# Retention in chunks worked as two spans of 64 tokens, with the outer product ahead of the scores and two GpSimd additions tied to the state

## The chip, the cores and the metric

One core of one Trainium2 chip runs the whole kernel in one launch. The metric is the device time in microseconds, the median of several runs. Five engines work side by side: TensorE (PE in the rows, its weight loads PEld), VectorE (DVE), ScalarE (ACT), GpSimd (POOL) and SyncE (SP, which issues DMAs). They meet only at semaphores.

## The reference, cut to what matters

A feed-forward block with 16 routed experts stands on both sides of an attention block; the change is inside the attention block, which has two layers over 4 sequences of 1024 tokens, 256 features, 16 heads of 16.

```
for i in range(2):
    ln_x = layer_norm(x, ln1_g[i], ln1_b[i])
    q, k, v, xo = split(ln_x @ proj_w[i] + proj_b[i], 4)
    scores = einsum('bhld,bhmd->bhlm', q, k) * D      # D[h,l,m] = gamma_h ** (l - m), 0 where m > l
    ret = einsum('bhlm,bhmd->bhld', scores, v)
    ret = (ret * silu(xo)) @ reto_w[i] + reto_b[i]
    x = x + ret
    h = layer_norm(x, ln2_g[i], ln2_b[i])
    x = x + gelu(h @ ffn1_w[i] + ffn1_b[i]) @ ffn2_w[i] + ffn2_b[i]
```

The decay is a power of the distance, so a sequence can be cut into pieces: inside a piece the scores are masked and multiplied with the values; what came before the piece is held in a state, the decayed sum of key times value, which is multiplied with the queries.

## The kernel before, in words

The 4096 tokens are 8 tiles of 512; with two layers there are 16 steps, and `step(a)` of each engine works on tile `a` and on the tile before it, `b`. Two steps make one sequence (`a.j` is 0 or 1); each tile is cut into four chunks `c` of 128 tokens, and `k` counts the eight chunks of a sequence. The order of work is written out by hand, engine by engine, in the five `step` functions; a semaphore says when each piece is done.

For chunk `c`, TensorE turns the keys (`turn_keys`, 2 transposes), makes the scores of the *next* chunk (`scores`, 8 matmuls that each use 32 rows of the array, so that four stand side by side in it), then `retain` (per half of the features 4 matmuls of the old state with the queries and 8 of the masked scores with the values, each 32 columns wide, again four side by side), then `outer` (8 matmuls, keys times values, the addition to the state), and then some blocks of the feed-forward layer of tile `b` (`feed_in`, 8 blocks a step, dealt out by `FEEDS`). The chunk matmuls are in full float32, and each leaves two rows in the trace; the others are split by `split3` into three fp32r products on the whole 128x128 array. A step ends with `turn_a`, `feed_out`, `project_out`, `project` of the next tile, its first `scores`, `turn_b` and `project_values`.

VectorE copies the turned keys out of PSUM (`copy_keys`), masks the scores (`masked`, four instructions a chunk), makes the new state (`update_state`: one product with a mask, two multiply-adds), applies the gate (`gate_result`) and makes the low parts of the feed-forward activations (`low_feed`). `turn_keys` of chunk `c+1` waits for the state of chunk `c`, since keys and products lie in the same PSUM bank, `m_ps`.

GpSimd makes `b_lo`, which `feed_in` of block 0 waits for, and right behind it adds two biases to the residual (`add_bias`).

Of the kernel before, what the change touches and what calls it, by code (L numbers as in the profile page):

```python
# [73 lines left out]
PH = QUAD // HD  # L74
WEIGHT_PIECES = 2 * KD + 3
# [1667 lines left out]
def retention(nc, h_sb, ident, eps, ins, x_dram, home, first_moe, next_moe, held, x_stored):  # L1743

    tag = "l"
    with ExitStack() as ctx:
# [28 lines left out]
        fresh = sb("fresh", [P, KD, P])  # L1775
        odd_probs = sb("probs1", [P, H * P])
# [4 lines left out]
        probs = [sb("probs0", [P, H * P]), odd_probs]  # L1781
# [15 lines left out]
        ret_ps, m_ps = rm_ps[:, 0, :], rm_ps[:, 1, :]  # L1797
# [14 lines left out]
        ret_done, gated_done, st_done, fresh_done, state_done = (  # L1812
            sem("ret_done"), sem("gated_done"), sem("st_done"), sem("fresh_done"), sem("state_done"))
# [64 lines left out]
        held.update({f"final{t}": (final_done, t + 1 if t < NT - 1 else NT - 1 + SUB) for t in range(NT)})  # L1878

# [9 lines left out]
        with nc.Block() as block:  # L1889
# [147 lines left out]
            def _(pool):  # L2037
# [23 lines left out]
                def add_bias(t, row, read, done):  # L2061
# [26 lines left out]
                def step(a):  # L2088
# [4 lines left out]
                    add_bias(a, 0, xn_done, based)  # L2093
# [21 lines left out]
                    add_bias(a, 1, xn2_done, fed)  # L2115
# [11 lines left out]
            def _(dve):  # L2127
# [87 lines left out]
                def masked(a, c, quads=range(NQ)):  # L2215
                    cc, w = SUB * a.n + c, 4 * P
                    if not isinstance(a.n, int) or cc > 1:
                        dve.wait_ge(ret_done, KD * (cc - 1))
# [6 lines left out]
                def copy_keys(n):  # L2225
                    dve.wait_ge(kturn_done, n + 1)
                    dve.tensor_copy(ks[:, :], m_ps[:, 0:D]).then_inc(ks_done, 1)

                def gate_result(a, c):
                    cc = SUB * a.n + c  # L2230
                    dve.wait_ge(ret_done, KD * (cc + 1))
                    part = slice(c * P, (c + 1) * P)
                    dve.tensor_tensor(gated[:, :, part], ret_ps[:, 0:KD * P].rearrange("p (g n) -> p g n", g=KD),
                                      gate[:, :, part], ALU.mult).then_inc(gated_done, 1)

                def update_state(batch, k):

                    dve.wait_ge(st_done, UPDATES * batch + k + 1)
                    part = m_ps[:, D:2 * D].rearrange("p (g n) -> p g n", g=KD)
                    if k == 0:  # L2240
                        dve.tensor_tensor(state[:, 0, :, :], part, own_head[:, :, :], ALU.mult).then_inc(state_done, 1)
                        return
                    dve.tensor_tensor(fresh[:, :, :], part, own_head[:, :, :], ALU.mult).then_inc(fresh_done, 1)
                    dve.wait_ge(fresh_done, (UPDATES - 1) * batch + k)
                    for g in range(KD):
                        last = dve.scalar_tensor_tensor(state[:, k % 2, g, :], state[:, (k - 1) % 2, g, :], state_decay[:, g:g + 1],
                                                        fresh[:, g, :], ALU.mult, ALU.add)
# [528 lines left out]
```

## Time and profile before

| | |
|---|---|
| median of 3 runs | 1406.06 us (1405.97 to 1408.61) |
| span of the profiled execution | 1579.5 us; no other time of it is given |
| TensorE busy | 1351.4 us, 86% of the span |
| VectorE busy | 1011.0 us, 64% |
| ScalarE, GpSimd busy | 614.6 us, 571.9 us |
| attention block alone, 408.5 to 1208 us of the span | TensorE busy 784.05 of 799.50 us |

The profiled execution is 173.4 us longer than the median. The profile has no second execution to say where this lies; the granted clock is 0.86 and 0.87 in the stretches of the two expert blocks and 1.00 in the attention block. In a timeline a row is a run of instructions of one kind: start, length to the end of the last, engine, line, what it writes and reads, count, and in brackets the idle time before it. Starts of matmul rows are recorded; their ends are modelled.

### The profile page before, as it was taken

Reading aid. Unit: us, or ns where it says so; the run is one execution under the profiler, and the core shown is the slowest. Engines: PE = TensorE matmul, PEld = TensorE weight load, DVE = VectorE, ACT = ScalarE, POOL = GpSimd, SP = SyncE. Lnnn points to the kernel's source line nnn. Section 1 sums busy time; section 2 is a strip of 40 time slices with the busy share of each in tenths; the row PEclk is TensorE's granted clock in tenths of the full one; section 3 lists DMA queues with packets and bytes.
Section 4 is the critical chain, followed back from the end, with each engine's and each line's share of the span. In section 5 each row is a group of like instructions: output and inputs, shape, how many; then the busy total and the mean of one; then the engine's idle time right before and its main releaser. Section 6 shows DMA issues by size and latency. Waiting matters only on the chain.

```text
span 1579.5 us, 30698 instructions
## 1 busy us (share of the span) xinstructions
PE 1351.4 (86%) x11824; PEld 1104.9 (70%) x11824; DVE 1011.0 (64%) x2391; ACT 614.6 (39%) x1034; POOL 571.9 (36%) x460
## 2 busy tenths in 40 slices
PE   6871968876999999999998999999999676496885
PEld 3461968644788888888886888888887446496753
DVE  5661536658977877777768778797787453253623
ACT  5630635422333433343344334424455262263410
POOL 0726033352342323224424443364343704304252
PEclk9975979989999999999999999999999788698998
DMA  9963559650000000000010000000002463355542
GB/s 326 372 213 122 174 175 321 206 190 23 28 2 2 1 2 1 1 2 32 8 58 1 1 15 2 15 15 14 2 28 89 167 229 131 124 181 171 156 150 90
DMA packets 113867, 151.63 MB, mean 96 GB/s; under 512 B 12224, under 2 KB 96192, under 8 KB 113728
## 3 DMA queue, kind: packets, MB, share of 16 engines
q1 hardware_dynamic: 99328, 114.02, 21.8%
q0 software_dynamic: 12288, 33.57, 6.6%
q8 instruction: 99, 1.62, 0.4%
q10 hardware_dynamic: 2112, 2.10, 0.4%
q14 instruction: 40, 0.33, 0.1%
HBM read 78.21 MB, written 71.43 MB: 95 GB/s over the span
## 4 chain that ended last, share of the span: by engine, by line
PE 53%; DVE 16%; another core or an unknown queue 8%; issue 2%; ACT 2%; POOL 0%; DVEq 0%; ACTq 0%
PE l_w_ps L83 8%; PE l_w_ps L85 7%; PE l_w_ps L84 7%; DVE l_probs L2221 4%; PE l_banks L2505 3%; PE l_rm_ps L2537 2%; PE l_banks L83 2%; PE l_banks L84 2%; PE l_banks L85 2%; DVE l_f_lo L2252 2%; PE l_rm_ps L2530 2%; DVE l_full L2174 1%; PE b_gu_ps L83 1%; PE b_t_ps L1284 1%
## 5 line engine op out<-in xcount | busy, mean ns | idle before, releaser
L2221 DVE TENSOR_TENSOR l_probs<-l_banks,l_past 128x512 f32<-128x512 f32 x256 | 160.1, 684 | 29.8 <-PE l_banks L2505 29.7
L1964 ACT ACTIVATE l_act_f<-l_w_ps,l_ffn_b 128x512 f32<-128x512 f32 x120 | 82.7, 690 | 169.0 <-PE l_w_ps L85 163.9
L83 PE MATMUL l_w_ps<-l_w_hi,l_f_hi 128*128 128x256 f32 x496 | 143.6, 290 | 2.6 <-DVE l_f_lo L2252 2.4
L84 PE MATMUL l_w_ps<-l_w_lo,l_f_hi 128*128 128x256 f32 x496 | 139.6, 281 | 0.0
L85 PE MATMUL l_w_ps<-l_w_hi,l_f_lo 128*128 128x256 f32 x496 | 139.5, 281 | 0.0
L2059 POOL TENSOR_TENSOR l_g_lo<-l_q,l_g_hi 128x1024 fp32r<-128x1024 f32 x16 | 39.1, 2447 | 266.9 <-ACT l_g_hi L1955 266.9
L813 POOL DMA_INDIRECT b_picked<-rows,b_pos_i x64 | 61.1, 955 | 137.4 <-DMA rows<-b_yb 88.5
L83 PE MATMUL l_w_ps<-l_b_hi,l_w_hi 128*128 128x512 f32 x240 | 102.2, 426 | 0.3 <-ACT l_f_hi L1965 0.3
L83 PEld LDWEIGHTS l_w_ps<-l_w_hi,l_f_hi 128*128 128x128 f32 x496 | 93.3, 188 | 8.8 <-issue 8.7
L2252 DVE TENSOR_TENSOR l_f_lo<-l_act_f,l_f_hi 128x512 fp32r<-128x512 f32 x128 | 85.9, 703 | 18.5 <-ACT l_f_hi L1965 18.4
L2046 POOL TENSOR_TENSOR l_q_wide<-l_q,l_pair_mask 128x1024 f32<-128x1024 f32 x32 | 60.1, 1899 | 103.7 <-DVE l_q L2189 100.0
L804 POOL DMA_INDIRECT rows<-a_xn,a_pos_i x64 | 66.3, 1036 | 83.9 <-DVE a_pos_i L969 64.9
L85 PE MATMUL l_w_ps<-l_b_hi,l_w_lo 128*128 128x512 f32 x240 | 94.7, 394 | 0.0
L84 PE MATMUL l_w_ps<-l_b_lo,l_w_hi 128*128 128x512 f32 x240 | 94.5, 394 | 0.0
L84 PEld LDWEIGHTS l_w_ps<-l_w_lo,l_f_hi 128*128 128x128 f32 x496 | 93.5, 188 | 0.0
L85 PEld LDWEIGHTS l_w_ps<-l_w_hi,l_f_lo 128*128 128x128 f32 x496 | 93.4, 188 | 0.0
L1965 ACT ACTIVATE l_f_hi<-l_w_ps,l_ffn_b 128x512 fp32r<-128x512 f32 x120 | 81.8, 681 | 0.0
L1943 ACT ACTIVATE l_std<-l_mv,eps 128x4 f32<-128x4 f32 x47 | 13.6, 298 | 174.4 <-DVE l_mv L2144 170.7
L2537 PE MATMUL l_rm_ps<-l_probs,l_v_wide 128*32 128x128 f32 x2048 | 78.9, 275 | 2.8 <-DVE l_v_wide L2210 2.8
L2067 POOL TENSOR_TENSOR x_sb<-x_sb,l_bias 128x1024 f32<-128x1024 f32 x32 | 77.2, 2414 | 0.0
L2505 PE MATMUL l_banks<-l_q_wide,l_kT 32*128 32x256 f32 x1024 | 74.2, 401 | 1.0 <-POOL l_q_wide L2046 1.0
L2154 DVE TENSOR_SCALAR l_xn<-x_sb,l_mv,l_rstd 128x256 f32<-128x256 f32 x128 | 69.8, 606 | 1.2
(432 smaller groups left out, 4053.0 us busy)
## 6 DMA issues: line engine op xcount, KB each, us to landing
rows<-a_zeros SPq DMA_DIRECT2D x14, 1024.0 KB, 10.7
a_xb<-rows SPq DMA_DIRECT2D x46, 256.0 KB
rows<-a_yb SPq DMA_DIRECT2D x46, 256.0 KB
b_xb<-rows SPq DMA_DIRECT2D x46, 256.0 KB
rows<-b_yb SPq DMA_DIRECT2D x46, 256.0 KB
a_w_in<-in_moe_w SPq DMA_DIRECT2D x15, 384.0 KB, 10.2
low_dram<-a_w_lo SPq DMA_DIRECT2D x15, 384.0 KB
b_w_lo<-low_dram SPq DMA_DIRECT2D x15, 384.0 KB
```

Source lines behind the costliest of these rows:

```text
L83: tensor.matmul(out, w_hi, x_hi, start=start, stop=False)
L84: tensor.matmul(out, w_hi, x_lo, start=False, stop=False)
L85: return tensor.matmul(out, w_lo, x_hi, start=False, stop=stop)
L804: pool.indirect_dma_start(own_rows[b], bass.IndirectOffsetOnAxis(ap=pos_i[:, b, k, c:c + 1], axis=0), normal(START[b] + c), None).then_inc ...
L1964: nc.scalar.activation(act_f[:, f, :], hidden_ps(b, f), ACT.Gelu, bias=ffn1_b[:, b.layer, f:f + 1]).then_inc(act_done, 1)
L1965: nc.scalar.activation(f_hi[:, f, :], hidden_ps(b, f), ACT.Gelu, bias=ffn1_b[:, b.layer, f:f + 1]).then_inc(f_hi_done, 1)
L2067: pool.tensor_tensor(tile, tile, bias[:, row:row + 1, :].broadcast_to([P, SUB, D]), ALU.add).then_inc(done, 1)
L2154: last = dve.tensor_scalar(dst(s), tile_of(t, s), mv[:, s, 0:1], rstd[:, s:s + 1], ALU.subtract, ALU.mult)
L2221: dve.tensor_tensor(probs[c % 2][:, r * w:(r + 1) * w].rearrange("p (h n) -> p h n", n=P), banks[:, r, :].rearrange("p (h n) -> p h n", n= ...
L2252: dve.tensor_tensor(f_lo[:, f, :], act_f[:, f, :], f_hi[:, f, :].bitcast(F32), ALU.subtract).then_inc(f_lo_done, 1)
L2505: last = pe.matmul(banks[:, r, g * PH * P:(g + 1) * PH * P], kT[rows, g, t], q_wide[rows, g, :, t], start=True, stop=True)
L2537: last = pe.matmul(ret_ps[r * QUAD:(r + 1) * QUAD, g * P:(g + 1) * P], v_wide[:, c, g * NQ + r, i:i + PH, :].rearrange("p i x -> p (i x)") ...
```

## The change

Each chunk of 128 tokens is worked as two spans (`h`) of 64. The scores of a span are masked within the span alone. What the second span needs of the first comes through a new buffer, `middle`, the state after the first span. So `outer` comes first in a chunk and gives two products; VectorE multiplies both with the mask in one instruction, makes `middle` from the old state and the first, and later the new state from `middle` and the second (`next_state`). Scores now use 32 rows by 64 columns of the array each, values and outer products 64 rows by 32 columns; the state matmuls keep 128 rows by 32 columns. All 8 chunks of a sequence now have an outer product. Keys, results and products are laid side by side in both PSUM banks of `rm_ps`; `turn_keys` of chunk `c+1` now waits for the gate of chunk `c`. The blocks of `feed_in` are dealt out as 3, 2, 2, 1 and stand between the parts of a chunk. Each bias addition also waits for a middle state: row 0 for that of chunk 2 of the same tile, row 1 for that of chunk 1 of the next tile.

```diff
+SPAN = P // 2
+SPANS = P // SPAN
...
-        ret_ps, m_ps = rm_ps[:, 0, :], rm_ps[:, 1, :]
+        ret_ps, keys_ps, m_ps = rm_ps[:, :, 0:P], rm_ps[:, :, P:2 * P], rm_ps[:, :, 2 * P:]
...
+        STATE_STEPS = 3
-        FEEDS = ((0,), (1, 2), (3, 4, 5), (6, 7))
+        FEEDS = ((0, 1, 2), (3, 4), (5, 6), (7,))
...
+        def state_steps(a, cc):
+            return STATE_STEPS * cc - a.batch
...
+                    if tile_now is not None:
+                        pool.wait_ge(state_step, state_steps(tile_now, SUB * tile_now.n + 2 - row) + 2)
...
-                    add_bias(a, 0, xn_done, based)
+                    add_bias(a, 0, xn_done, based, a)
...
-                    add_bias(a, 1, xn2_done, fed)
+                    add_bias(a, 1, xn2_done, fed, after(a, 1) if more else None)
...
-                        dve.tensor_tensor(probs[c % 2][:, r * w:(r + 1) * w].rearrange("p (h n) -> p h n", n=P),
-                                          banks[:, r, :].rearrange("p (h n) -> p h n", n=P),
-                                          past[:, :].unsqueeze(1).broadcast_to([P, 4, P]), ALU.mult).then_inc(probs_done, 1)
+                        dve.tensor_tensor(probs[c % 2][:, r * w:(r + 1) * w].rearrange("p (h n) -> p h n", n=SPAN),
+                                          banks[:, r, 0:w].rearrange("p (h n) -> p h n", n=SPAN),
+                                          past[:, 0:SPAN].unsqueeze(1).broadcast_to([P, 4, SPAN]), ALU.mult).then_inc(probs_done, 1)
...
+                def middle_state(a, cc, k):
+                    dve.wait_ge(st_done, cc + 1)
...
+                    dve.tensor_tensor(fresh[:, 0:n, :, :], products[:, 0:n, :, :], own, ALU.mult).then_inc(state_step, 1)
+                    dve.wait_ge(state_step, state_steps(a, cc) + 1)
+                    for g in range(KD):
+                        last = dve.scalar_tensor_tensor(middle[:, g, :], state[:, (k - 1) % 2, g, :], state_decay[:, g:g + 1],
+                                                        fresh[:, 0, g, :], ALU.mult, ALU.add)
+                    last.then_inc(state_step, 1)
+
+                def next_state(a, cc, k):
+                    dve.wait_ge(state_step, state_steps(a, cc) + 2)
+                    for g in range(KD):
+                        last = dve.scalar_tensor_tensor(state[:, k % 2, g, :], middle[:, g, :], state_decay[:, g:g + 1],
+                                                        fresh[:, 1, g, :], ALU.mult, ALU.add)
+                    last.then_inc(state_step, 1)
...
-                            last = pe.matmul(banks[:, r, g * PH * P:(g + 1) * PH * P], kT[rows, g, t], q_wide[rows, g, :, t],
-                                             start=True, stop=True)
...
+                        for h in range(SPANS):
+                            keys, own = slice(h * SPAN, (h + 1) * SPAN), span(c, h)
...
+                                last = pe.matmul(banks[keys, r, g * PH * SPAN:(g + 1) * PH * SPAN], kT[rows, g, own], q_wide[rows, g, :, own],
+                                                 start=True, stop=True)
...
+                    if c > 0:
+                        pe.wait_ge(gated_done, cc)
...
+                def retain(a, c, k):
+                    cc = SUB * a.n + c
+                    pe.wait_ge(state_step, state_steps(a, cc) + (2 if k == 0 else 1))
+                    for g in range(KD):
+                        for i in range(PH):
+                            for h in range(SPANS):
+                                keys = slice(h * SPAN, (h + 1) * SPAN)
+                                for r in range(NQ):
...
+                                    pe.matmul(ret_ps[r * QUAD:(r + 1) * QUAD, h, g * SPAN:(g + 1) * SPAN],
+                                              v_wide[keys, c, g * NQ + r, i:i + PH, :].rearrange("p i x -> p (i x)"),
+                                              probs[c % 2][keys, head * SPAN:(head + 1) * SPAN],
+                                              start=(g + i == 0), stop=(g == KD - 1 and i == PH - 1 and k + h == 0))
+                    for h in range(SPANS):
+                        if k + h == 0:
+                            continue
+                        if h == 1:
+                            pe.wait_ge(state_step, state_steps(a, cc) + 2)
+                        for g in range(KD):
...
+                                w = middle[:, g, quad] if h else state[:, (k - 1) % 2, g, quad]
+                                last = pe.matmul(ret_ps[quad, h, g * SPAN:(g + 1) * SPAN], w, q[:, g, span(c, h)], start=False, stop=(g == KD - 1))
+                    last.then_inc(ret_done, 1)
```

TensorE, one chunk in the middle of a step, before (`L2516` turns keys, `L2505` scores, `L2530` state with queries, `L2537` scores with values, `L2548` outer product, `l_b_hi` a feed-forward block):

```order
L2516 MATMUL l_rm_ps<-ident,l_kT 128x128 [waits l_state_done]
L2516 MATMUL l_rm_ps<-ident,l_kT 128x128
L2505 MATMUL l_banks<-l_q_wide,l_kT 128x256 [waits l_probs_done] x4
L2505 MATMUL l_banks<-l_q_wide,l_kT 128x256 x4
L2530 MATMUL l_rm_ps<-l_q,l_state 32x128 [waits l_state_done,l_v_done,l_gated_done]
L2530 MATMUL l_rm_ps<-l_q,l_state 32x128 x3
L2537 MATMUL l_rm_ps<-l_probs,l_v_wide 32x128 [waits l_probs_done] x4
L2537 MATMUL l_rm_ps<-l_probs,l_v_wide 32x128 x4
L2530 MATMUL l_rm_ps<-l_q,l_state 32x128 x4
L2537 MATMUL l_rm_ps<-l_probs,l_v_wide 32x128 x8
L2548 MATMUL l_rm_ps<-l_v_wide,l_ks 32x128 [waits l_ks_done]
L2548 MATMUL l_rm_ps<-l_v_wide,l_ks 32x128 x7
```

The same place after (`L2562` outer product, `L2538` scores, `L2577` values, `L2590` states, `L2550` the next chunk's keys):

```order
L2562 MATMUL l_rm_ps<-l_v_wide,l_ks 32x128 [waits l_ks_done,l_v_done]
L2562 MATMUL l_rm_ps<-l_v_wide,l_ks 32x128 x15
L2538 MATMUL l_banks<-l_q_wide,l_kT 64x128 [waits l_probs_done] x4
L2538 MATMUL l_banks<-l_q_wide,l_kT 64x128 x12
L2577 MATMUL l_rm_ps<-l_probs,l_v_wide 32x64 [waits l_probs_done,l_state_step]
L2577 MATMUL l_rm_ps<-l_probs,l_v_wide 32x64 [waits l_probs_done] x3
L2577 MATMUL l_rm_ps<-l_probs,l_v_wide 32x64 x28
L2590 MATMUL l_rm_ps<-l_q,l_state 32x64 x8
L2590 MATMUL l_rm_ps<-l_q,l_middle 32x64 [waits l_state_step]
L2590 MATMUL l_rm_ps<-l_q,l_middle 32x64 x7
```

The outer product moved from last to first, the values now wait for a step of the state, and 40 matmuls of a chunk became 80 of half the size or half the array, with the same two transposes besides.

VectorE at the same place after (`L2259` both products with the mask, `L2262` the middle state, `L2231` masks, `L2247` gate, `L2269` the new state, `L2237` copy of the next keys, `L2275` low parts):

```order
L2259 TENSOR_TENSOR l_fresh<-l_rm_ps,l_own_head 128x512 [waits l_st_done]
L2262 SCALAR_TENSOR_TENSOR l_middle<-l_state,l_state_decay,l_fresh 128x128 [waits l_state_step]
L2262 SCALAR_TENSOR_TENSOR l_middle<-l_state,l_state_decay,l_fresh 128x128
L2231 TENSOR_TENSOR l_probs<-l_banks,l_past 128x256 [waits l_scores_done,l_ret_done]
L2231 TENSOR_TENSOR l_probs<-l_banks,l_past 128x256 [waits l_scores_done] x3
L2247 TENSOR_TENSOR l_q<-l_rm_ps,l_gate 128x2x128 [waits l_ret_done]
L2269 SCALAR_TENSOR_TENSOR l_state<-l_middle,l_state_decay,l_fresh 128x128 [waits l_state_step]
L2269 SCALAR_TENSOR_TENSOR l_state<-l_middle,l_state_decay,l_fresh 128x128
L2237 COPY l_ks<-l_rm_ps 128x256 [waits l_kturn_done]
L2275 TENSOR_TENSOR l_f_lo<-l_act_f,l_f_hi 128x512 [waits l_f_hi_done] x3
```

Before, the copy of the keys stood first, then four masks of 128x512, the product of 128x256, one pair of multiply-adds and the gate. The product now stands ahead of the masks, behind the low parts of the chunk before it, and there are two pairs of multiply-adds.

## Rows read from the trace of the kernel before

**Rows 1.** The page: span, and busy time of the engines.
```profile
span 1579.5 us, 30698 instructions
PE 1351.4 (86%) x11824; PEld 1104.9 (70%) x11824; DVE 1011.0 (64%) x2391; ACT 614.6 (39%) x1034; POOL 571.9 (36%) x460
```

**Rows 2.** Windows: stretch, length, busy us and count by engine, PEclk, DMA.
```profile
0.00:354.20 354.20, 255.47 (x1491) 202.49 (x1491) 182.68 (x445) 150.59 (x285) 129.61 (x136) 0.86 0.70 234
354.20:408.50 54.30, 42.06 (x437) 30.46 (x436) 49.70 (x126) 13.15 (x18) 15.55 (x10) 0.91 0.13 40
408.50:1208.00 799.50, 784.05 (x8337) 661.58 (x8330) 613.51 (x1431) 310.92 (x459) 302.36 (x188) 1.00 0.05 14
567.38:620.63 53.25, 52.79 (x557) 44.48 (x556) 40.74 (x100) 19.86 (x29) 16.08 (x9) 1.00 0.01 1
620.63:673.18 52.55, 51.90 (x559) 44.00 (x558) 40.64 (x98) 19.86 (x29) 16.24 (x9) 1.00 0.01 2
```

**Rows 3.** Timeline of TensorE, first chunk of a step and start of the second.
```profile
625.51 0.38 PE L2516 MATMUL l_rm_ps<-ident,l_kT 128*128 128x128 f32 x2
625.82 1.15 PE L2505 MATMUL l_banks<-l_q_wide,l_kT 32*128 32x256 f32 x16
626.90 0.43 PE L2530 MATMUL l_rm_ps<-l_q,l_state 128*32 128x128 f32 x8
627.14 0.62 PE L2537 MATMUL l_rm_ps<-l_probs,l_v_wide 128*32 128x128 f32 x16
627.58 0.40 PE L2530 MATMUL l_rm_ps<-l_q,l_state 128*32 128x128 f32 x8
627.80 0.62 PE L2537 MATMUL l_rm_ps<-l_probs,l_v_wide 128*32 128x128 f32 x16
628.23 0.62 PE L2548 MATMUL l_rm_ps<-l_v_wide,l_ks 128*32 128x128 f32 x16
628.78 0.50 PE L83 MATMUL l_w_ps<-l_b_hi,l_w_hi 128*128 128x512 f32 x1
629.12 0.39 PE L84 MATMUL l_w_ps<-l_b_lo,l_w_hi 128*128 128x512 f32 x1
...
631.10 0.44 PE L2516 MATMUL l_rm_ps<-ident,l_kT 128*128 128x128 f32 x2 [0.66 <-DVE l_state L2246]
```

**Rows 4.** Windows on L2530 alone: matmuls begun by 35 ns and by 170 ns.
```profile
626.89:626.92 0.04, 0.03 (x4) 1.00 0.00 0
626.89:627.06 0.17, 0.16 (x8) 1.00 0.00 0
```

**Rows 5.** Waits of TensorE's weight loads, 420 to 1180 us: total, times, longest.
```profile
PEld l_rm_ps L2516 <- DVE l_state L2246: 8.1, 7, 1.9
PEld l_rm_ps L2516 <- DVE l_state L2241: 3.7, 7, 0.5
```

**Rows 6.** Timeline of VectorE in the same step.
```profile
623.07 1.52 DVE L2174 TENSOR_SCALAR l_full<-l_rm_ps,l_norm 128x512 f32<-128x512 f32 x2
624.51 1.28 DVE L2221 TENSOR_TENSOR l_probs<-l_banks,l_past 128x512 f32<-128x512 f32 x2
625.70 1.28 DVE L2210 TENSOR_TENSOR l_v_wide<-l_w_ps,l_v_b 128x512 f32<-128x512 f32 x2
...
630.08 0.97 DVE L2246 SCALAR_TENSOR_TENSOR l_state<-l_state,l_state_decay,l_fresh 128x128 f32<-128x128 f32 x2
...
631.57 0.42 DVE L2227 COPY l_ks<-l_rm_ps 128x256 f32<-128x256 f32 x1 [0.20 <-PE l_rm_ps L2516]
...
642.59 1.89 DVE L2252 TENSOR_TENSOR l_f_lo<-l_act_f,l_f_hi 128x512 fp32r<-128x512 f32 x3
```

**Rows 7.** Timeline of ScalarE and GpSimd in the same step.
```profile
624.63 1.06 ACT L1951 ACTIVATE l_b_hi<-l_full 128x1024 fp32r<-128x1024 f32 x1 [3.20 <-DVE l_full L2174]
...
625.76 2.38 POOL L2055 TENSOR_TENSOR l_b_lo<-l_full,l_b_hi 128x1024 fp32r<-128x1024 f32 x1 [5.66 <-ACT l_b_hi L1951]
...
630.79 2.48 POOL L2067 TENSOR_TENSOR x_sb<-x_sb,l_bias 128x1024 f32<-128x1024 f32 x1
```

More of the change, by code:

```diff
@@ L2236, in update_state, with spans @@
-                def update_state(batch, k):
-                    dve.wait_ge(st_done, UPDATES * batch + k + 1)
-                    part = m_ps[:, D:2 * D].rearrange("p (g n) -> p g n", g=KD)
+                    def spans(of):
+                        return of[:, :, part].rearrange("p g (h n) -> p g h n", h=SPANS)
+                    dve.tensor_tensor(spans(gated), ret_ps.rearrange("p h (g n) -> p g h n", g=KD), spans(gate),
+                                      ALU.mult).then_inc(gated_done, 1)
@@ L2240, in update_state @@
+                def middle_state(a, cc, k):
+                    dve.wait_ge(st_done, cc + 1)
+                    products = m_ps.rearrange("p h (g n) -> p h g n", g=KD)
                     if k == 0:
-                        dve.tensor_tensor(state[:, 0, :, :], part, own_head[:, :, :], ALU.mult).then_inc(state_done, 1)
+                        dve.tensor_tensor(fresh[:, 1, :, :], products[:, 1, :, :], own_head[:, :, :], ALU.mult).then_inc(state_step, 1)
+                        dve.tensor_tensor(middle[:, :, :], products[:, 0, :, :], own_head[:, :, :], ALU.mult).then_inc(state_step, 1)
@@ L2500, in scores @@
                             pe.wait_ge(k_done, KD * (a.n + 1))
-                        for r in range(NQ):
-                            if g == 0 and c > 0:
-                                pe.wait_ge(probs_done, NQ * (cc - 1) + r + 1)
-                            rows = slice(r * QUAD, (r + 1) * QUAD)
-                            last = pe.matmul(banks[:, r, g * PH * P:(g + 1) * PH * P], kT[rows, g, t], q_wide[rows, g, :, t],
-                                             start=True, stop=True)
-                            if g == KD - 1:
-                                last.then_inc(scores_done, 1)
@@ L2517, in turn_keys, with outer @@
                     last.then_inc(kturn_done, 1)
-                def retain(a, c, k, n):
+                def outer(a, c, k):
                     cc = SUB * a.n + c
-                    if not isinstance(a.n, int) or cc > 0:
-                        pe.wait_ge(gated_done, cc)
                     pe.wait_ge(v_done, 2 * a.n + c // 2 + 1)
-                    if k > 0:
-                        pe.wait_ge(state_done, n)
+                    pe.wait_ge(ks_done, cc + 1)
                     for g in range(KD):
-                        if k > 0:
+                        for h in range(SPANS if k < UPDATES else 1):
+                            keys = slice(h * SPAN, (h + 1) * SPAN)
+                            for r in range(NQ):
+                                quad, w = slice(r * QUAD, (r + 1) * QUAD), slice(g * P + r * QUAD, g * P + (r + 1) * QUAD)
+                                last = pe.matmul(m_ps[quad, h, g * P:(g + 1) * P], ks[keys, w],
+                                                 v_wide[keys, c, g * NQ:(g + 1) * NQ, 0::PH, :], start=True, stop=True)
+                    last.then_inc(st_done, 1)
@@ L2541, in retain @@
-                        last.then_inc(ret_done, 1)
-                def outer(c, n):
-                    pe.wait_ge(ks_done, n + 1)
-                    for g in range(KD):
-                        for r in range(NQ):
-                            quad, w = slice(r * QUAD, (r + 1) * QUAD), slice(g * P + r * QUAD, g * P + (r + 1) * QUAD)
-                            last = pe.matmul(m_ps[quad, D + g * P:D + (g + 1) * P], ks[:, w],
-                                             v_wide[:, c, g * NQ:(g + 1) * NQ, 0::PH, :], start=True, stop=True)
-                    last.then_inc(st_done, 1)
+                                w = middle[:, g, quad] if h else state[:, (k - 1) % 2, g, quad]
@@ L2648, in step @@
                         feed_out(b)
-                    project_out(a, last_state)
+                    project_out(a)
                     project(after(a, 1), b)
```

145 lines of the change are left out of this document (74 added, 71 removed).

## The prediction

> **What bounds the kernel now.** I read the page first: TensorE is busy 86% of the span, VectorE 64% [rows 1]. Shares over a whole span say little, so next come windows by stage. The attention block runs from about 408.5 to 1208 us, and there TensorE is busy 784.05 of 799.50 us at full granted clock; a single step is 53.25 or 52.55 us long and TensorE is busy 52.79 and 51.90 of it. VectorE is busy some 40.7 us of a step, and no other engine 20 [rows 2]. The reader should see one engine that hardly ever stands still, and then ask what it does with its time, because busy time says neither that its array is full nor that it is at its peak. The timeline of one chunk answers that. The scores are 16 rows that start at 625.82; the next group starts at 626.90. The values are 16 rows in 0.44 us (627.14 to 627.58) and 16 more in 0.43, and the outer product 16 rows from 628.23 [rows 3]. The narrow windows show how: four matmuls have begun by 35 ns, and eight by 170 ns [rows 4]. So four tiles of the array work side by side and each holds a set of four for 0.44/4 = 0.109 us. That is a quarter of the array each, and for the values half of what is multiplied is the zeroed upper half of a 128x128 mask.
>
> The block has a few real waits: turning keys waited for the state 8.1 us in seven steps and 3.7 in seven others [rows 5]; one of them, 0.66 us, is in the rows at 631.10 [rows 3]. In the first step, 354.2 to 408.5 us, it is the other way round: VectorE is busy 49.70 of 54.30 us [rows 2].
>
> The profiled execution has a span of 1579.5 us and the median of the runs is 1406.06. Its granted clock is 1.00 in the attention block and 0.86 in the expert block before it [rows 2]. I take what the change does in the attention block from this span, and subtract it from the median as it is, since I have no row that says the attention block is longer here than in a plain run.
>
> **The change, part by part.** Negative numbers are time won, for the 64 chunks of the run.
>
> *Scores.* Before, 8 matmuls, 16 rows: four sets of 0.216 us, 0.87 in all (the 1.08 from 625.82 to 626.90 less what the change of tile shape costs, below). After, 16 matmuls of half the columns on tiles of 32x64, eight side by side: four sets of 0.109 = 0.44. Won: 64 x 0.43 = 27.5 us.
>
> *Values.* 32 rows before, 0.87 us [rows 3]. After, 64 rows with 64 columns each, so 0.055 a set, and eight side by side: 8 sets = 0.44. Won: 64 x 0.43 = 27.5 us.
>
> *Both of these rest on eight tiles at once*, which the trace doesn't show. It shows four side by side in rows of the array (32*128, scores) and four in columns (128*32, the rest) [rows 3], and that four begin within 35 ns [rows 4]. Bounds: nothing won in the values and the outer product twice as long (below, as a rival), or the full factor. I take the full factor, since each of the two directions is shown by itself. The Trainium skill says in "TensorE: Matmul & The Clock Gate", Part 3, that row and column tiles compose, up to 16 at once; no row of this trace has both, and it speaks for the same end.
>
> *States and outer products.* States: twice the matmuls of half the columns, four side by side: 0.44 as before. Outer: twice the matmuls on half the rows, eight side by side: 0.44 as before. New are the middle state in the first chunk of a sequence, 8 x 0.22 us, and a key turn and half an outer product in the last, 8 x 0.44. Lost: 5.3 us.
>
> *Changes of tile shape.* Rows 3 let them be priced. From keys to scores: two transposes end at 625.51 + 0.22 = 625.73, scores start at 625.82: 0.09. From scores to the state: four sets of 0.216 from 625.82 give 626.68, but it is 626.90: 0.22, of which I count 0.10 to the entry and 0.12 to the exit. From the outer product back to the whole array: 16 sets of 0.109 from 626.90 give 628.65, but the next starts at 628.78, and the one behind it at 629.12 where 0.23 is its normal distance: 0.13 + 0.11 = 0.24. So it costs 0.1 to 0.24 us each time. In a step there are ten more such changes: in the first and the last chunk one more return to the whole array (0.24) and one more entry (0.12) each, and six between narrow shapes (0.10 each). That is 1.3 us a step, 16 steps: lost, 21 us. Bounds: 11 us if narrow shapes change for nothing, 38 if all cost 0.24.
>
> *Key turns.* They no longer wait for the state but for the gate of the chunk before, with a feed-forward block of 6 x 0.23 = 1.4 us in between. That hides it: after `retain` ends VectorE may still have four masks of 0.35 us and the gate of 0.42, half of which ran already. Won: 8.1 + 3.7 = 11.8 us [rows 5]. If the cover went, a wait of some 0.6 us a chunk would be back.
>
> *A new wait: values behind the product.* `retain` now waits for the product with the mask. In chunks 0 and 3 a feed-forward block lies in between. In chunks 1 and 2 only the scores do. The last outer matmul ends 0.27 us after its start, VectorE follows 0.03 to 0.09 later (631.10 + 0.44 = 631.54, copy at 631.57 [rows 3, 6]), and the product is 128x512, like the masks, 0.68 us (two end 1.28 after the first starts [rows 6]). With a semaphore back that is 1.1 us; TensorE fills it with 0.44 of scores and two changes of shape, 0.7. Left: 0.4 us. In chunk 2 the product stands behind three low parts, 1.89 us [rows 6], that start only when the keys are copied: 0.2 more. Behind the waiting matmul stands all of TensorE's work. Lost: 1.0 us a step, 16 us; bounds 0 and 32.
>
> *A new wait: block 0.* Only chunk 0's outer product is now ahead of the first block, and that block needs `b_lo`. VectorE scaled at 623.07 behind two masks; these shrink from 0.60 to 0.33 each, so scaling, ScalarE's b_hi (624.63) and GpSimd's b_lo (625.76 + 2.38 = 628.14) move up by 0.55 to 627.6 [rows 6, 7]. TensorE, with two shorter scores and `retain` moved behind the block, could be there at about 626.8: keys turned at 625.1, scores to 626.0, outer product to 626.6, change of shape. On the way it also waits for the key copy, which stands behind the values' additions (1.28 us [rows 6]). Together 0.8 us a step, 15 steps: lost, 12 us; bounds 5 and 20.
>
> *VectorE.* Masks: 4 x 0.27 less a chunk; product 0.26 more; a second pair of multiply-adds 0.55 more. It is 0.3 us lighter a chunk. This lies beside TensorE except in the first step, where VectorE's chain sets the pace: some 1 us in three of its chunks, won 3 us.
>
> *GpSimd.* The two additions (2.4 us each) start later by waiting; their results are needed only by the sums after `feed_out` and `project_out`, over 30 us on, so they cost nothing. While one ran, a pair of multiply-adds took 0.97 us [rows 6, 7]; such a pair is now free of it where TensorE waits for `middle`. If an addition did come under the pair, the cost would be 0.4 us where nothing hides it.
>
> **Sum:** -27.5 - 27.5 + 5.3 + 21 - 11.8 + 16 + 12 - 3 = -15.5 us, which takes 1406.06 to about **1390 us** (and this profile's span to about 1564).
>
> **The rivals.**
>
> *Tiles that share a column group take turns* (the other side). Values and outer products of both spans write the same 32 partitions from different rows of the array. If the two row halves are served in turn, the values stay at 0.87 us (+27.5) and the outer products double (60 full ones x 0.44 = +26). That gives 1390 + 54 = 1444 us. For it: no row here has both kinds of tiling at once. Against it: scores already write the same partitions from four row groups in 0.216 us a set [rows 3]. It decides as soon as these two parts lose more than 30% of those 54 us. Chance 0.14.
>
> *The instructions come too slowly.* A full chunk has 160 matmul rows of the narrow kinds instead of 80. If 0.109/4 = 27 ns a row were not the array's pace but that of the supply, 160 rows would take 4.4 us and not 1.76: +2.6 us a chunk, about 1390 + 160 = 1550 us. Against it: four begin within 35 ns [rows 4], but these may have stood ready. Chance 0.04. The same would follow from a rule of the Trainium skill ("TensorE: Matmul & The Clock Gate", Part 1): starts of matmuls never come closer than about 25 ns, however short they are; by that page, an estimate, the chunk would come to 4.0 us and the whole to about 1530. By that rule, the trace does not agree: it has four starts in 35 ns.
>
> *The new waits eat the gain.* If the values wait 0.9 us in both chunks, with the product or with masks still ahead of it on VectorE, against 0.4 and 0.6 this is 0.8 us a step, 13 us more; with the wait for block 0 at its upper bound it is 8 more still: 1399 to 1412, about 1404 in the middle. For it: VectorE is at 40.7 of 53 us and now stands in TensorE's path four times a step instead of once. Chance 0.20.
>
> *More is won.* Waits of a quarter of a microsecond and cheap changes between narrow shapes: 8 + 10 us better, 1372 to 1382. Chance 0.12.
>
> *The forecast*, 1383 to 1398: chance 0.50.
>
> **How the numbers follow.** The predicted time is that of the forecast. The range of 1375 to 1430 leaves out the two slow rivals (0.18) and a little at the fast end. About 0.2% is what a measurement of this kernel tells from no change. Faster: forecast 0.50, more won 0.12, and 0.02 of the eaten gain, 0.64. Within 0.2%: 0.11 of the eaten gain. Slower: its other 0.07 and the two slow rivals, 0.25.
>
> **What the profile after would show.** A steady step of about 52.0 us (before 52.9). Scores: 32 rows from first to last start in 0.5 us instead of 0.9. Values: 64 rows in 0.44 to 0.5 us; 0.87 or more speaks for tiles in turn, 1.7 for the supply. Masks of 128x256 at about 0.42 us. No wait of key turns on the state; values waiting for L2259 twice a step by 0.4 us; block 0 waiting for `b_lo`. GpSimd's additions some 10 and 17 us into a step, nobody waiting for them. The forecast is wrong if any of these misses by half a microsecond in every chunk, since 64 chunks make that 32 us.

## The result and the profile after

The kernel after takes 1426.85 us (median of 4 runs, 1424.01 to 1427.84), the one before 1406.01 (1405.49 to 1408.61): a ratio of 1.0147, 95% interval 1.013 to 1.0164. It is 21 us slower; 1390 us was forecast.

The page of after, the lines that answer to [rows 1], the queue that brings TensorE's instructions (packets, MB), and two of its costliest groups:

```profile
span 1422.2 us, 41198 instructions
PE 1303.6 (92%) x16960; PEld 1070.8 (75%) x16960; DVE 1027.8 (72%) x2543; ACT 616.1 (43%) x1034; POOL 573.8 (40%) x460
...
q8 instruction: 139, 2.28, 0.6%
...
L2081 POOL TENSOR_TENSOR l_pool_carrier<-l_norm 128x1 f32<-128x1 f32 x56 | 10.7, 196 | 231.2 <-DVE l_middle L2262 201.8
...
L2577 PE MATMUL l_rm_ps<-l_probs,l_v_wide 64*32 64x64 f32 x4096 | 57.5, 227 | 19.2 <-DVE l_fresh L2259 14.1
```

TensorE has 16960 rows instead of 11824. The same queue brought 99 packets and 1.62 MB before, so it grew with TensorE's rows. Windows of after: the first step, the attention block, two steady steps (compare [rows 2]; the columns are the same):

```profile
286.00:345.00 59.00, 41.44 (x730) 29.94 (x717) 49.01 (x133) 11.89 (x16) 13.23 (x10) 0.80 0.12 37
345.00:1140.00 795.00, 754.49 (x12957) 632.92 (x12963) 617.32 (x1536) 305.88 (x452) 291.46 (x176) 0.99 0.04 11
510.01:563.22 53.21, 51.05 (x885) 42.94 (x877) 41.50 (x108) 19.85 (x30) 16.14 (x9) 1.00 0.01 2
563.22:616.43 53.21, 51.25 (x884) 43.13 (x876) 41.45 (x107) 19.83 (x30) 16.16 (x9) 1.00 0.01 2
```

A steady step takes 53.2 us where 52.0 was forecast and 52.9 was the mean before. Timeline of TensorE in after, the place of [rows 3] and the two chunks behind it, without the feed-forward rows:

```profile
513.80 0.38 PE L2550 MATMUL l_rm_ps<-ident,l_kT 128*128 128x128 f32 x2
514.11 0.69 PE L2538 MATMUL l_banks<-l_q_wide,l_kT 32*64 32x128 f32 x32
515.17 0.67 PE L2562 MATMUL l_rm_ps<-l_v_wide,l_ks 64*32 64x128 f32 x32 [0.36 <-DVE l_ks L2237]
516.34 0.47 PE L85 MATMUL l_w_ps<-l_b_hi,l_w_hi 128*128 128x512 f32 x1 [0.50 <-POOL l_b_lo L2063]
...
517.89 0.86 PE L2577 MATMUL l_rm_ps<-l_probs,l_v_wide 64*32 64x64 f32 x64
518.68 0.43 PE L2590 MATMUL l_rm_ps<-l_q,l_middle 128*32 128x64 f32 x16
...
522.85 0.69 PE L2538 MATMUL l_banks<-l_q_wide,l_kT 32*64 32x128 f32 x32
523.77 0.86 PE L2577 MATMUL l_rm_ps<-l_probs,l_v_wide 64*32 64x64 f32 x64 [0.23 <-DVE l_fresh L2259]
524.56 0.43 PE L2590 MATMUL l_rm_ps<-l_q,l_state 128*32 128x64 f32 x16
...
530.26 0.86 PE L2577 MATMUL l_rm_ps<-l_probs,l_v_wide 64*32 64x64 f32 x64 [0.64 <-DVE l_fresh L2259]
531.04 0.43 PE L2590 MATMUL l_rm_ps<-l_q,l_state 128*32 128x64 f32 x16
531.29 0.39 PE L2590 MATMUL l_rm_ps<-l_q,l_middle 128*32 128x64 f32 x10
532.10 0.31 PE L2590 MATMUL l_rm_ps<-l_q,l_middle 128*32 128x64 f32 x6 [0.42 <-issue]
```

The reader should see three things. The values hold TensorE for 0.79 us (517.89 to 518.68), change of tile shape included; the forecast had 0.44, and 0.10 for that change. The waits are those forecast: 0.36 and 0.50 at block 0, 0.23 and 0.64 for the product. And in the middle of a run of equal rows stands a pause that no engine ends ("issue"): the sixteen rows on `l_middle` start up to 531.46 and go on at 532.10. Windows on the value rows alone, of the chunk at 523.77:

```profile
523.76:524.02 0.26, 0.25 (x32) 0.25 (x33) 1.00 0.00 0
523.76:524.43 0.67, 0.66 (x64) 0.66 (x64) 1.00 0.00 0
```

Half of the 64 rows start in 0.24 us and the other half takes 0.40. The next kind of row follows 0.15 us behind the last.

The first profile of before was 173 us above its median; the run before_again below gave one with a span of 1404.8 us. By its first transposes of a step, the time lies here:

| stretch | before, us | after, us |
|---|---|---|
| up to the first `turn_a` | 262.2 | 260.3 |
| from there to the first `turn_b` (first step) | 82.5 | 89.5 |
| six steady steps | 317.0 | 319.1 |
| the three steps in which the second layer's weights are split | 166.5 | 171.1 |
| five steady steps | 265.8 | 266.8 |
| last step | 47.2 | 49.7 |
| what is left | 263.7 | 265.7 |

### The profile page after: what moved, and what is told of

Read it like the earlier page. It is cut to its first block, busy times and chain, and to the rows that moved or that the text cites. A ratio compares the mean times of both kernels' runs of the same rounds, so it can differ in the third digit from the quotient of the medians.

```text
span 1422.2 us, 41198 instructions
## 1 busy us (share of the span) xinstructions
PE 1303.6 (92%) x16960; PEld 1070.8 (75%) x16960; DVE 1027.8 (72%) x2543; ACT 616.1 (43%) x1034; POOL 573.8 (40%) x460
## 3 DMA queue, kind: packets, MB, share of 16 engines
q8 instruction: 139, 2.28, 0.6%
## 4 chain that ended last, share of the span: by engine, by line
PE 61%; DVE 13%; issue 3%; ACT 3%; POOL 3%; SPq 1%; DMA 0%; DVEq 0%; ACTq 0%
PE l_w_ps L85 9%; PE l_w_ps L87 8%; PE l_w_ps L86 8%; PE l_rm_ps L2577 3%; PE l_banks L85 2%; PE l_banks L87 2%; PE l_banks L86 2%; POOL l_b_lo L2063 2%; DVE l_f_lo L2275 2%; PE l_rm_ps L2590 2%; DVE l_state L2269 2%; PE b_gu_ps L85 2%; DVE l_fresh L2259 1%; PE b_t_ps L417 1%; PE l_rm_ps L2562 1%
## 5 line engine op out<-in xcount | busy, mean ns | idle before, releaser
L85 PE MATMUL l_w_ps<-l_b_hi,l_w_hi 128*128 128x512 f32 x240 | 106.4, 443 | 7.3 <-POOL l_b_lo L2063 6.5
L2081 POOL TENSOR_TENSOR l_pool_carrier<-l_norm 128x1 f32<-128x1 f32 x56 | 10.7, 196 | 231.2 <-DVE l_middle L2262 201.8
L1951 ACT ACTIVATE l_std<-l_mv,eps 128x4 f32<-128x4 f32 x47 | 13.6, 296 | 189.1 <-DVE l_mv L2154 188.9
L2231 DVE TENSOR_TENSOR l_probs<-l_banks,l_past 128x256 f32<-128x256 f32 x256 | 91.7, 418 | 4.0 <-PE l_banks L2538 4.0
L2275 DVE TENSOR_TENSOR l_f_lo<-l_act_f,l_f_hi 128x512 fp32r<-128x512 f32 x128 | 85.7, 711 | 0.0
L2577 PEld LDWEIGHTS l_rm_ps<-l_probs,l_v_wide 64*32 64x32 f32 x4096 | 45.7, 107 | 39.9 <-DVE l_fresh L2259 23.2
L2577 PE MATMUL l_rm_ps<-l_probs,l_v_wide 64*32 64x64 f32 x4096 | 57.5, 227 | 19.2 <-DVE l_fresh L2259 14.1
```

The source lines that it names most:

```text
L85: tensor.matmul(out, w_hi, x_hi, start=start, stop=False)
L2275: dve.tensor_tensor(f_lo[:, f, :], act_f[:, f, :], f_hi[:, f, :].bitcast(F32), ALU.subtract).then_inc(f_lo_done, 1)
L2577: pe.matmul(ret_ps[r * QUAD:(r + 1) * QUAD, h, g * SPAN:(g + 1) * SPAN], v_wide[keys, c, g * NQ + r, i:i + PH, :].rearrange("p i x -> p (i ...
```

## The experiments

**before_again.** No edit.

> The kernel before, profiled a second time. If the 173 us that its first profile had over the median lay outside the attention block, as the prediction assumed, the span is now about 1404 us and a steady step again 52.5 to 53.3 us. If they lay partly inside it, steady steps are now shorter than that, and the sum was made against wrong rows.

1406.62 us, span 1404.8; steady steps 52.5 and 53.3 us.

```profile
292.00:340.00 48.00, 38.37 (x402) 29.11 (x403) 44.90 (x114) 10.00 (x14) 10.98 (x7) 0.89 0.11 32
340.00:1135.00 795.00, 779.14 (x8269) 655.66 (x8268) 609.15 (x1415) 310.86 (x459) 297.90 (x184) 1.00 0.04 11
```

The same stretch of 795 us holds the same work as in [rows 2]. By the first transposes of the steps, 55 of the 173 us lay ahead of the attention block, 111 behind it, and 10 in its first step (92.9 us there, 82.5 here); the fifteen other steps together differ by 2 us. So their rows were the right ones for the sum.

**values_doubled**, on the kernel after:

```diff
-                    for g in range(KD):
+                    for again in (1, 0):
+                      for g in range(KD):
```

> The kernel after, with the 64 value rows of every chunk issued twice; the second pass overwrites the first with the same numbers. After, a burst of 64 rows runs its first 32 in 0.24 us and is done at 0.64 us, the same in every chunk. Supply theory (the rows behind the 32 that stood ready come at the pace of the instruction supply): the second pass shows no fast part, its 64 rows take 0.6 to 0.8 us, 38 to 51 us in all: 1465 to 1478 us. Rival (something at the change from the first half of the features to the second): the second pass begins with 32 fast rows again and repeats the pattern, 0.64 us or more. Rival (once a chunk): 0.44 us for the second pass, 1455 us.

1514.99 us (ratio 1.0775, 1.0748 to 1.0801), 88 us above after. An undisturbed burst:

```profile
543.96 1.48 PE L2578 MATMUL l_rm_ps<-l_probs,l_v_wide 64*32 64x64 f32 x128
545.37 0.43 PE L2591 MATMUL l_rm_ps<-l_q,l_middle 128*32 128x64 f32 x16
```

Start times of every sixteenth row of that burst, in ns from the first: 0, 137, 267, 481, 626, 794, 927, 1107, and the last at 1267. Only the first 32 rows are fast; rows 65 to 128 take 0.64 us, 10 ns each, and show no fast part. That is the supply theory's pattern. The cost is 1.38 us a chunk, though, and more than any theory said: the rest is pauses. From 340 to 1200 us, in 43 places inside the bursts of narrow rows two starts lie 0.2 us or more apart (up to 2.5), 48.5 us in all.

**before_doubled**, the control: state and value rows of the kernel before issued twice, by the same edit.

> The kernel before, with the state and value rows of every chunk (16 and 32, each 128 columns) issued twice; the second pass overwrites the first with the same numbers. A control for the doubled values of the kernel after, where 64 more rows a chunk cost 0.63 us in the rows and as much again in pauses of 0.5 to 1.1 us inside the burst. Supply theory: here a row occupies the array for 27 ns, longer than the supply needs, so the 48 extra rows cost 1.31 us a chunk (0.87 in a chunk without a state), 80 us in all, about 1487 us, and no burst holds a pause. Rival (a burst that is long pauses whatever its rows are): pauses of half a microsecond and more appear here too, 1510 us and above.

1494.33 us, one run, 88 us above before (80 expected).

```profile
535.12 0.62 PE L2538 MATMUL l_rm_ps<-l_probs,l_v_wide 128*32 128x128 f32 x16
535.55 0.40 PE L2531 MATMUL l_rm_ps<-l_q,l_state 128*32 128x128 f32 x8
535.77 0.62 PE L2538 MATMUL l_rm_ps<-l_probs,l_v_wide 128*32 128x128 f32 x16
```

The burst is twice as long and keeps its pace of 27 ns a row (0.43 us for 16), and in the same stretch of the trace it has no pause at all. So it takes more than a long burst to make a pause. The 8 us above the expected 80 were not followed up.

**values_order**, on after: the loops over `i` and `g` in the values exchanged.

> The kernel after, with the loops over the head of a pair and over the half of the features exchanged in the values: rows 33 to 64 are now the second heads of both halves instead of the second half of the features. Supply theory: nothing changes, 32 rows in 0.24 us and the last at 0.64 us, 1427 us. Rival (it is the half of the features that costs): the slow stretch moves to another place or is cut in two.

1426.37 us (one run); the fast part again ends with the 32nd row and the last row starts at 0.642 us. Which half of the features a row belongs to does not matter, its place in the burst does.

**half_values**, on after. It leaves out the second head of each pair in the values.

```diff
-                        for i in range(PH):
+                        for i in (0,):
```

> The kernel after, in which the values leave out the second head of each pair: 32 value rows a chunk instead of 64, on the same eight tiles, all else as it was. Supply theory (32 rows stand ready and run at the array's pace, the other 32 take 0.40 us, and the pauses of half a microsecond and more come because the stream of instructions is used up too fast): a burst takes 0.24 us instead of 0.64, 26 us less in 64 chunks, and most of the 8 us of pauses go too: 1393 to 1400 us. Array theory (the burst costs 0.44 us as forecast, the rest is elsewhere): half of it goes, 0.22 us a chunk, 14 us, 1413 us, and the pauses stay.

1400.92 us (ratio to before 0.9965, 0.995 to 0.9981), 26 us below after. The supply theory's burst is there, with the wait ahead of it longer than in after:

```profile
523.97 0.46 PE L2577 MATMUL l_rm_ps<-l_probs,l_v_wide 64*32 64x64 f32 x32 [0.98 <-DVE l_fresh L2259]
524.36 0.43 PE L2590 MATMUL l_rm_ps<-l_q,l_state 128*32 128x64 f32 x16
```

All 32 rows start in 0.24 us, in each of the 64 chunks. 64 x 0.40 = 25.6 us is the whole difference. The run also takes work away: at the pace of the fast half the 32 rows that are gone would have taken 0.22 us a chunk, 14 us in all (the expectation's array theory), so 12 of the 26 us are what the slow pace costs. Pauses fell from 9 us in 14 places to 3 in 4, and waits for the product rose from 11.5 to 18.0 us, so these two cancel.

**free_bias**, on after: both bias additions without the wait for a middle state.

```diff
-                    add_bias(a, 0, xn_done, based, a)
+                    add_bias(a, 0, xn_done, based, None)
-                    add_bias(a, 1, xn2_done, fed, after(a, 1) if more else None)
+                    add_bias(a, 1, xn2_done, fed, None)
```

> The kernel after, with GpSimd's two bias additions no longer tied to the middle states. Theory A (the additions cost nothing, as predicted): 1427 us, within 3. Theory B (they hold up what stands behind them on GpSimd in the steps that also split the second layer's weights, and slow VectorE while TensorE waits for its product): the waits of 1.64 and 1.08 us in the seventh step shrink, and the time falls by 4 to 8 us, to 1419 to 1423 us.

1425.67 us (ratio 1.0132, 1.0111 to 1.0154), not to be told from after. The three steps of the weight split fall from 171.1 to 165.3 us, but the five behind them rise by 2.0 and the last by 1.7. Theory B holds for its three steps alone; the total is theory A's. VectorE in after, in the first of them, and GpSimd beside it:

```profile
691.59 3.64 DVE L2269 SCALAR_TENSOR_TENSOR l_state<-l_middle,l_state_decay,l_fresh 128x128 f32<-128x128 f32 x2
695.16 0.41 DVE L2237 COPY l_ks<-l_rm_ps 128x256 f32<-128x256 f32 x1
695.49 3.13 DVE L2275 TENSOR_TENSOR l_f_lo<-l_act_f,l_f_hi 128x512 fp32r<-128x512 f32 x2
...
690.31 2.40 POOL L2077 TENSOR_TENSOR x_sb<-x_sb,l_bias 128x1024 f32<-128x1024 f32 x1
692.66 4.81 POOL L2049 TENSOR_TENSOR l_wp_lo<-l_wp,l_wp_hi 128x1024 fp32r<-128x1024 f32 x2
```

A pair of multiply-adds of 0.61 us takes 3.64 while GpSimd works from 690.3 to 697.5 without a break, and TensorE then waits 1.63 us for the keys and 1.08 for the product.

**pieces_first**, on after: the three `split_piece` groups moved ahead of `add_bias(a, 0, ...)`.

> The kernel after, with GpSimd's pieces of the weight split in three steps ahead of the first bias addition, which keeps its wait. If the held bias addition delays the pieces, and these then slow VectorE beside TensorE's chunk work: the three steps come back to what they are with free additions (165 us instead of 171), 1421 us. Rival: nothing stands behind the pieces and VectorE is slowed by them wherever they lie: 1427 us.

1430.77 us (1.0182, 1.0158 to 1.0206), no gain: the three steps take 171.9 us. The addition now waits behind pieces that wait for ScalarE, and one piece still lies beside the chunk. The rival holds.

**scores_ahead**, on pieces_first:

```diff
-        FEEDS = ((0, 1, 2), (3, 4), (5, 6), (7,))
+        FEEDS = ((0, 1), (2, 3), (4, 5), (6, 7))
...
+                        turn_keys(a, c)
+                        if c + 1 < SUB:
+                            scores(a, c + 1)
+                        elif feeds:
+                            feed_in(a, b, feeds.pop(0))
                         outer(a, c, k)
+                        if feeds:
+                            feed_in(a, b, feeds.pop(0))
                         retain(a, c, k)
                         if feeds:
                             feed_in(a, b, feeds.pop(0))
```

> As the run with the pieces first, and besides the next scores stand ahead of the outer product in every chunk, and a feed-forward block between the outer product and the values (two blocks in each chunk). The waits of the values for the product (0.23 and 0.64 us a step) and the pause behind it in the third chunk (0.42) should go, against two more changes of tile shape a step (0.36 each): 0.5 us a step better than with the pieces first, 8 us in all, 1413 us. Rival: the waits come back at the key copy, same time as with the pieces first, 1421 us. If the changes of shape cost more than counted: 1425 us or more.

1417.99 us (1.0091, 1.0069 to 1.0113), 13 us below pieces_first where 8 were expected. The run changes the order and the dealing of the blocks at once, so the gain can't be split between the two. Steady steps are 52.2 us instead of 53.2. Its waits of TensorE from 350 to 1120 us (total, times, longest):

```profile
PE l_rm_ps L2562 <- DVE l_ks L2237: 9.5, 18, 1.7
PE l_w_ps L85 <- POOL l_b_lo L2063: 6.5, 13, 0.5
```

The 11.5 us of waits for the product are gone. The pauses fell to 2 us in 5 places. I read this as the feed-forward block, with 0.23 us a row, giving the supply its time between the bursts.

**ahead_freed**, on scores_ahead: pieces back in their place, and no wait of the additions in the four steps around the weight split.

> As the run scores_ahead, but with the weight pieces behind the first bias addition as in the kernel after, and with the waits of the additions taken away in the four steps around the weight split only. In the kernel after the free additions took 5.8 us off these three steps (171.1 to 165.3) and gave 3.7 back in later ones. Theory (the wait costs only where there are pieces to split): 5 us below the 1418 of scores_ahead, 1412 to 1413 us. Rival (the pieces cost the same wherever they lie): 1418 us.

1409.97 us (1.0033, 1.002 to 1.0045): 8 us below scores_ahead (5 expected), 165.7 us for the three steps. This is the new scheme with its waits and collisions mostly repaired, and it is still 0.3% slower than before.

**before_product**, on the kernel before: `turn_keys` waits for the product and not for the whole state (the product is the last read of that bank).

```diff
-                    if not isinstance(n, int) or n > 0:
-                        pe.wait_ge(state_done, n)
+                    products = n - a.batch - (1 if k > 0 else 0)
+                    if k == 1:
+                        pe.wait_ge(state_done, n)
+                    elif products > 0:
+                        pe.wait_ge(fresh_done, products)
```

> The kernel before, in which the keys of the next chunk are turned behind the product alone (which is the last read of that bank) and no longer behind the whole state. Theory: the waits of key turns, 11.8 us in the first profile, shrink by the two multiply-adds, some 0.5 us in each place that waited: 4 to 8 us faster, 1398 to 1402 us. Rival: the same time is waited right behind, by the state matmuls or the key copy: 1406 us.

1400.23 us (0.9951, 0.9932 to 0.997), as the theory said.

**even_feeds**, on before_product: `FEEDS = ((0, 1), (2, 3), (4, 5), (6, 7))`.

> The kernel before, keys turned behind the product as in the run before_product, and the feed-forward blocks dealt out 2, 2, 2, 2 instead of 1, 2, 3, 2. Theory: the remaining wait of the key turns goes (two blocks cover the state in the first chunk), and in every second step, where the output of the feed-forward layer now waits 1.35 us for the low parts, part of that goes too, since they are made earlier: 1391 to 1397 us. Rival: the waits for the low parts stay, since the last two blocks are where they were: 1400 us.

1388.15 us (0.9874, 0.9859 to 0.9889): better than both kernels, by 18 and 39 us, and 3 us better than the theory's best.

```profile
395.80:448.00 52.20, 51.87 (x561) 44.54 (x557) 40.71 (x99) 19.83 (x29) 16.08 (x9) 1.00 0.01 2
448.00:499.40 51.40, 51.40 (x559) 44.12 (x555) 40.52 (x97) 19.83 (x29) 16.23 (x9) 1.00 0.01 1
```

In the second of these steps TensorE is busy all the time.

**early_feeds**: the same dealt out 2, 2, 3, 1.

> The run even_feeds with the blocks dealt out 2, 2, 3, 1: the seventh block is made one chunk earlier, the eighth alone stands ahead of the last values. In even_feeds every second step still waits 0.75 us more than the other in the output of the feed-forward layer, for low parts. Theory: that goes, 8 x 0.75 = 6 us, 1382 us. Rival: VectorE now makes the eighth low part ahead of the last gate and the gated result comes late: 1388 us or more.

1389.37 us (0.988, 0.9863 to 0.9896), no gain; steps of 52.1 and 51.4 became 52.0 and 51.4. Theory and rival are each half right: from `turn_a` to `turn_b` the longer step fell from 25.28 to 24.93 us, 0.35 of the 0.75, but 0.2 came back ahead of `turn_a`.

## Why the prediction was wrong

**The step that failed: "I take the full factor"**, the term of -27.5 us for the values. Eight tiles do work side by side, and for 32 rows they keep the pace of the sum: 0.055 us for a set of eight. Then the rows come no faster than one in 12 ns (0.40 us for 32). The values took 0.89 us a chunk before (0.87 in the sum). They take 0.65 now, and the change of shape behind them 0.13: 0.24 won where 0.43 was counted. Against the 0.44 of the sum that is 0.21 us a chunk, 13 to 14 us in 64 chunks. half_values gives 12 for the same thing. values_doubled shows that all that follows the first 32 rows comes at the slow pace, and before_doubled that the number of rows alone costs nothing more. The weight loads aren't the limit either: the first 32 of a burst start in 0.19 us. That leaves the supply of instructions as the reading that fits all these runs, and it is argued by exclusion; which part of the supply sets 10 to 12 ns a row, no run shows.

**The rival "the instructions come too slowly" was the right mechanism at the wrong size.** I priced it at 27 ns a row everywhere, which the four starts in 35 ns [rows 4] seemed to exclude, and gave it 0.04. Those rows had stood ready, as I wrote, but the consequence wasn't drawn: a supply between 7 and 27 ns a row hurts only the one burst that is faster than it. The scores and outer products, at 0.109 us for eight rows (13.6 ns each), just pass.

**Pauses were in no term.** Inside rows of one kind there are 14 places, 9 us, from the first step on. Two more stand between values and state rows (0.44 and 0.59 us from start to start, where 0.15 is normal): together some 10 us. They come from the supply too, as the last section shows, so the same step failed twice.

**Scores, -27.5**: right. Thirty-two rows start in 0.425 us, sixteen took 0.774; with the last set 0.53 against 0.99, 0.46 won a chunk.

**"Tiles that share a column group take turns"**: excluded. The outer product's sets of eight follow at 0.109 us, and the first values at 0.055.

**Changes of tile shape, States and outer product**: nearly right. The way back to the whole array costs 0.24 us (518.68 + 4 x 0.055 = 518.90, first full rows at 519.04 and 519.38), an entry 0.1. Between two narrow shapes it is 0.13 to 0.14 where 0.10 was counted, some 3 us in the run.

**Key turns, -11.8**: the waits are gone as forecast in steady steps, but they were worth less. 11.8 us was the idle time of the weight loads [rows 5]. By the starts of the transposes, 1.07 and 0.48 us behind the row before them in before_again where 0.23 is normal, it was 1.1 us in two steps, some 9 us in all. In the first step they wait for the gate, 1.9 us.

**New waits, +28**: right. 0.23 + 0.64 = 0.87 us a step for the product against 1.0, and 0.36 + 0.50 = 0.86 for block 0 against 0.8. So they are not what ate the gain.

**A gain that I didn't see.** In the kernel before, `feed_out` waits for low parts in every second step: from `turn_a` to `turn_b` 24.54 and 25.87 us in turn. After, it is 24.09 in each; 0.44 of this are the shorter scores. That is 1.35 us in seven or eight steps, some 10 us, which came with the new order of the blocks and not with the spans. even_feeds gets part of it in the old scheme.

**VectorE's first step, -3**: wrong, it is 7 us longer. From the first `turn_a` to the first `turn_b` TensorE is busy 70.03 of 89.53 us at a mean granted clock of 0.87 (between its two levels, 1.2 and 2.4 GHz); in before_again it is busy 68.34 of 82.48 us at 0.92. So 5.4 of the 7 us are idle time, and the rest is busy time at a lower clock. In it the weight split of VectorE (two instructions) takes 4.51 us beside GpSimd's `g_lo`, where it took 2.35 before.

**GpSimd's additions, 0**: right as a total (free_bias, 1 us), by accident: 5.8 us lost in the steps of the weight split, 3.7 won elsewhere.

Together, in rounded terms: -15.5 + 14 (values) + 10 (pauses) + 3 (shapes) + 3 (key turns) - 2 (scores) - 10 (low parts) + 10 (first step) + 6 - 4 (additions) = +14.5. The two profiles, 1422.2 and 1404.8 us, are 17.4 us apart, the medians 21. So some 3 us of the profiles' difference have no name, and the sum is rough, since terms of the first step are in it twice. 24 of the 30 us by which this sum misses the forecast are the supply's, values and pauses. The last step is 2.5 us longer (0.75 of it a pause); what the rest of it is was not tried, nor why the first step's two engines collide just there.

## What to carry to other kernels

Halving matmuls so that more tiles stand side by side doubles the rows for the same work. Before counting the gain, divide the time of each burst by its rows: a row that needs less than 10 to 12 ns is paid at that (here), beyond the 32 rows that stand ready. Long rows ahead of a burst don't speed up its second half (the burst at 517.89 stands behind them and takes 0.642 us like the others), but bursts spread apart have fewer pauses (scores_ahead). And look for a wait that asks for more than it needs (the state for the product), and for the order of filler blocks, first: in this kernel these two gave 18 us with no change of the algorithm.

## What the runs showed of the hardware

TensorE's instructions have a pace of their own. Fast rows (each a weight load and a matmul) come in sets of eight every 0.055 us, 6.9 ns a row, for the first 32 of a burst, and at 10 to 12 ns behind them. The Trainium skill says in "TensorE: Matmul & The Clock Gate", Part 1, that starts never come closer than about 25 ns; by this rule, the trace does not agree: 64 rows start in 0.642 us, 10 ns each.

The pauses lie on a grid. In the kernel after, counted in TensorE rows and from the second on, the 14 are 127, 885, 127, 1644, 885, 3286, 1771, 1012, 759, 127, 885 and 886 rows apart, all multiples of about 126.5 within a row or two. One row is two instructions, so that is one place in about 253 of the instructions that leave a row; waits leave none. The page's instruction queue fits: 2.28 MB in 139 packets is 16.4 KB a packet, and from the third pause to the last there are 97 packets and 12267 rows, 126.5 each. The Trainium skill, "Runtime: NRT & Kernel Launch", "Instruction fetch mechanics", says that an engine's instructions are fetched in blocks of 16 KiB, 256 instructions, and that crossing a boundary is mostly hidden. With the block size the trace agrees. Hidden it is in the kernel before, which has no pause, but not where bursts of fast rows follow each other: 0.25 to 1.0 us from start to start in after, up to 2.5 in values_doubled.

Why one boundary costs a microsecond and the next nothing is in the trace as well, which has start and length of every packet. Each of the 16 pauses of after ends 1.2 to 1.5 us after a packet of that queue has ended, 2.2 to 2.7 us after it began. The same grid gives the other boundaries: 98 from the third pause to the last, and at none of them does the row behind it start less than 1.2 us after its packet has ended. So TensorE stands when it reaches a boundary earlier than that, and the time it takes to get there decides. The 80 rows behind a packet's start take as little as 1.1 us in after and 0.8 in values_doubled, but never under 3.8 in before_again nor under 2.2 in before_doubled, and these two have no pause. That TensorE waits for the block is read from these times; what makes a packet start when it does is not shown.

GpSimd slows some of VectorE's instructions and not others. In after, a pair of multiply-adds took 0.61 us alone, 1.52 beside one addition (at 525.94) and 3.64 beside three operations in a row (at 691.59). Over the attention block of after, one multiply-add of the new state has a median of 0.34 us alone and of 1.26 wholly beside GpSimd, while masks (0.42), gate (0.42 to 0.43) and key copy (0.42) stay as they are; these three read from PSUM, the multiply-adds don't. GpSimd's additions take 2.4 us whatever VectorE does, but its `g_lo` took 3.30 us beside VectorE's weight split in before_again, where 2.39 is normal.
